# Two steps' products with the values issued together in causal attention, over three buffers of exponentials

## The reference

```python
scores = jnp.einsum('bqhd,bkhd->bhqk', q, k)
scores = scores + jnp.einsum('bqr,bkr->bqk', q_rope, k_rope)[:, None]
scores = scores / scale
scores = jnp.where(causal[None, None], -jnp.inf, scores)
w = jax.nn.softmax(scores, axis=-1)
attn = jnp.einsum('bhqk,bkhd->bqhd', w, v).reshape(Bb, Tt, D_MODEL)
return attn @ W_o
```

## Time and profile before

| | us |
|---|---|
| median of 3 runs | 2069.44 (2067.35 to 2071.24) |
| profiled execution, its own time | 2063.16 |
| its span, first to last instruction | 2061.4 |
| attention, first to last exponential | 235.6 to 1146.7 |
| TensorE busy over the span | 1628.2 |
| VectorE busy over the span | 1153.2 |
| ScalarE busy over the span | 876.3 |

### The profile page before, as it was taken

How to read it: one execution, slowest core, us unless ns; L and a number is a source line. 1 busy time by engine, 2 the same in 40 slices (tenths; PEclk the granted TensorE clock), 3 DMA queues, 4 the chain that set the end, 5 groups by cost and what they waited for, 6 DMA issues and landing times. The chain is left out here.

```text
span 2061.4 us, 32062 instructions
## 1 busy us (share of the span) xinstructions
PE 1628.2 (79%) x12596; PEld 758.6 (37%) x12596; DVE 1153.2 (56%) x3013; ACT 876.3 (43%) x1186; POOL 351.5 (17%) x414
## 2 busy tenths in 40 slices
PE   7954579999999999999999276401887967888889
PEld 5421122333333333333333152201343434566566
DVE  3815779787878778786870034500444565311466
ACT  2420245666666666666667103301454533311132
POOL 2512780000000000000000040174221200300011
PEclk9985799999999999999999686655999988999989
DMA  7487440303030120404000130025665410584011
GB/s 255 156 176 167 135 135 22 78 27 78 14 79 26 49 56 27 70 22 78 27 27 27 68 133 0 13 105 140 146 160 140 130 47 1 204 289 166 5 36 52
DMA packets 94213, 183.85 MB, mean 89 GB/s; under 512 B 12656, under 2 KB 60912, under 8 KB 93040
## 3 DMA queue, kind: packets, MB, share of 16 engines
q1 hardware_dynamic: 73024, 110.91, 21.1%
q0 software_dynamic: 19376, 68.41, 10.1%
q10 hardware_dynamic: 1664, 2.49, 0.3%
HBM read 123.31 MB, written 58.37 MB: 88 GB/s over the span
## 5 line engine op out<-in xcount | busy, mean ns | idle before, releaser
L885 ACT ACTIVATE at_pr<-ps 128x1024 f32<-128x1024 f32 (+3 forms) x640 | 546.7, 894 | 349.4 <-PE ps L825 220.3
L918 DVE TENSOR_REDUCE at_mx<-ps 128x1 f32<-128x512 f32 x768 | 489.1, 685 | 149.2 <-PE ps L777 141.0
L915 DVE CUSTOM_DVE_ANT_0 at_seen<-ps,later 128x384 bf16<-128x384 f32 (+3 forms) x512 | 229.2, 486 | 16.1 <-issue 10.7
L825 PE MATMUL ps<-bq,bk 64*128 64x512 f16 (+3 forms) x1280 | 224.0, 347 | 0.0
L822 PE MATMUL ps<-sqk 64*128 64x512 f16 (+3 forms) x1280 | 172.6, 348 | 13.4 <-DMA sqk<-at_mr 13.4
L822 PE MATMUL ps<-at_sqk 64*128 64x512 f16 (+3 forms) x1280 | 171.2, 346 | 6.4 <-DMA at_sqk<-at_mr 5.7
L777 PE MATMUL ps<-sqk 64*128 64x512 f16 (+3 forms) x640 | 120.7, 374 | 61.4 <-DVE at_mx L918 29.5
L719 POOL DMA_DIRECT2D d_o<-at_oc x32 | 17.3, 540 | 807.8 <-ACT at_oc L876 785.1
L801 PE MATMUL ps<-at_pr,vl 128*32 128x512 f32 (+3 forms) x1280 | 150.5, 542 | 0.0
L801 PE MATMUL ps<-at_pr,at_vl 128*32 128x512 f32 (+3 forms) x1280 | 150.0, 541 | 0.1
L777 PE MATMUL ps<-at_sqk 64*128 64x512 f16 (+3 forms) x640 | 114.7, 355 | 19.9 <-DVE at_mx L918 8.1
(11 more groups left out here) (264 smaller groups left out, 2367.7 us busy)
## 6 DMA issues: line engine op xcount, KB each, us to landing
mi_tz<-d_z SPq DMA_DIRECT2D x32, 1024.0 KB, 7.0
ex_w<-d_w POOLq DMA_DIRECT2D x23, 768.0 KB, 6.5
d_rows<-at_nil POOLq DMA_DIRECT2D x32, 379.5 KB, 3.0
ex_xr<-d_rows SPq DMA_DIRECT2D x23, 512.0 KB, 8.8
d_va<-st_va SPq DMA_DIRECT2D x8, 1024.0 KB, 4.9
d_o<-at_oc POOLq DMA_DIRECT2D x32, 256.0 KB, 2.3
at_pw<-in_w POOLq DMA_DIRECT2D x24, 256.0 KB, 3.1
d_w<-at_ph POOLq DMA_DIRECT2D x24, 256.0 KB, 2.4
```

Of the source, the lines that this page charges most:

```text
L825: ins = pe.matmul(ps[:, 2 * f + r, off:CH], g.bk[half[r], b, k], g.bq[half[r], b, q], start=False, stop=t < 0)
L885: act.activation(pr[:, n % 2, f, :, off:CH], ps[:, 2 * f:2 * f + 2, off:CH], ACT.Exp, scale=INV_SCALE).then_inc(exp_done[f], 1)
L915: ins = dve.tensor_tensor_reduce(seen[:, turn, r, 0:n], src, g.later[:, CH - n:CH], 1.0, LOWEST, ALU.add, ALU.max, dst)
L918: ins = dve.tensor_reduce(dst, src, AX.X, ALU.max)
```

## The change

`pr` gets a third buffer. A step's buffer is now the number of the step over all units, modulo three. TensorE issues no product with the values in odd steps; in an even step it issues those of the two steps before, one behind the other, in the place where the one of the step before stood. In step 0 these are the last two of the unit before. ScalarE waits for the product of three steps back. The spreading of the maxima and everything else stays.

```diff
+    PR = 3
...
-        pr = sb("pr", [P, 2, 2, 2, CH])
+        pr = sb("pr", [P, PR, 2, 2, CH])
...
-                                    pr[:, n % 2, h // 2, h % 2, off:CH], start=(kb == 0),
+                                    pr[:, (u * NS + n) % PR, h // 2, h % 2, off:CH], start=(kb == 0),
...
                     if s == 0 and not first:
+                        weighted(*before, NS - 2)
                         weighted(*before, NS - 1)
-                    if s >= 1:
+                    if s >= 2 and s % 2 == 0:
+                        weighted(grp, b, s - 2)
                         weighted(grp, b, s - 1)
...
                 if last:
+                    weighted(grp, b, NS - 2)
                     weighted(grp, b, NS - 1)
...
-                    act.wait_ge(pv_done[n % 2], u * (NS // 2) + n // 2 + 1)
+                    step = u * NS + n
+                    if step >= PR:
+                        act.wait_ge(pv_done[(step - PR) % 2], (step - PR) // 2 + 2)
...
-                        act.activation(pr[:, n % 2, f, :, off:CH], ps[:, 2 * f:2 * f + 2, off:CH], ACT.Exp,
+                        act.activation(pr[:, step % PR, f, :, off:CH], ps[:, 2 * f:2 * f + 2, off:CH], ACT.Exp,
```

## The result

| | before | after |
|---|---|---|
| median us | 2070.34 (4 runs, 2067.35 to 2080.03) | 2143.76 (4 runs, 2138.19 to 2150.14) |
| ratio | | 1.035 (95% interval 1.032 to 1.038) |
| profiled execution's span | 2061.4 | 2148.4 |
| attention, first to last exponential | 911.0 | 986.2 |

A forecast was written before the change was run, and what follows sets the result against it. TensorE and VectorE were taken to share the bound, step by step. Six middle units at +9.8 us give +59, the first +11, the last +12: +82 us, so 2151 us is predicted, range 2118 to 2193.

The forecast's parts named there:

- Price of the surroundings: TensorE in attention: pair to pair 1.18 us with only scores between; a second product behind the first costs 0.90.
- parts 1 to 3: Odd steps gain 0.01 to 0.13 us, even steps pay 0.90; middle unit +8.0 for wide pairs, +2.1 and +0.6 for narrower.
- part 4: Step 9, without maxima: transposition 0.5 us earlier, then 0.9 and 0.1 paid in step 10, +0.5 in all.
- part 5: Steps with short scores and no second pair, whose 256-wide product was not covered: together -1.3 us a middle unit.
- part 6: Transposition for the next unit starts 0.3 us earlier, the next unit's step 0 pays 0.2: taken -0.1.
- part 7: Third buffer of exponentials and ScalarE's wait three steps back: nothing is queued longer, cost 0.
- First unit: First of attention's eight units (one group of heads of one batch), first seven odd steps saturated: +11 us.
- Last unit: Attention's eighth unit, no maxima to make ahead: about +3 in steps 0 to 8, +9 from step 9, +12 us.
- Rival A: Borders of the products: half of 320 save 0.25 us each in switches, 40 us faster, 2029 us; chance 0.07.
- Rival B: Slack takes it up: TensorE's gain in odd steps balances the even steps' 0.90 us, no change, 2069; chance 0.04.
- Rival C: Second product pays its entire fixed part (+34, 2185 us) or granted clock falls (2177); chance 0.09 together with Rival D.
- Rival D: An exponential waits for its buffer and the scores behind it wait too, adding time; chance under 1 in 50.

The follow-up runs named there:

- the clean base: The changed kernel with its products put back, one in each step, third buffer kept: last unit 94.1 us, whole 2063.35 us, ratio to before 1.001.
- the kernels with both cuts: Kernels before and after, with reductions over 32 columns and exponentials over 128, the rest left out: 1979.30 and 1989.63 us, ratios to before 0.958 and 0.964.

## Why the prediction was right

The forecast was 2151 us, +82; measured 2143.76, +73, and attention +75.2. The kernel is slower by the mechanism named: the product was taken off VectorE's time, and ScalarE's in the last unit.

*Price of the surroundings.* Pair to pair 1.17 with nothing between (1.18 forecast), 2.16 over two products (2.21). The second product costs 2.16-1.31 = 0.85 us, its columns alone (0.86 in the forecast); with the border I had taken 0.90. So the border between two products costs nothing that shows. By the weight-load rule of the Trainium skill (TensorE: Matmul & The Clock Gate, Part 3), that a load overlaps running matmuls only where the row groups differ, I had put it at 0.1 us. The measurement decides against this use of it: both products use all rows, and the block of sixteen runs through.

*Odd and even steps (parts 1 to 3).* Forecast +0.80 a period with wide pairs, measured 0.72 to 0.77 in nine of ten and 0.80 in one: 0.85-0.14 = 0.71 and a little saturation. With 384 columns 0.68, 0.60 and 0.68 for 0.70; step 29 0.60 for 0.6. Together about 10.0 for 10.7.

*Step 9 (part 4).* +0.48 for +0.5. *Steps 15, 27, 35 (part 5).* -0.67, -0.02, -0.46, together -1.15 for -1.3. *End of a unit (part 6).* -0.2 for -0.1 (+0.54 in steps 37 and 38, -0.74 in 39 and the next unit's first). *Third buffer (part 7).* 0 for 0, by its own run. Middle unit: +9.1 for +9.8.

*First unit:* +10.9 for +11. That it fits so well is luck: by the scatter of this unit (139.9 and 141.3 with the old order, 150.8 and 149.2 with the new) the cost lies anywhere from 8 to 11, and the clock granted in it was 0.95 to 0.98 in all kernels, with no tie to the order.

*Last unit:* +10.0 against the clean base (+9.4 against the profile of before) for +12. This is the term furthest off. Steps 0 to 8 cost +2.9 for 3, its full periods 0.73 to 0.79 for 0.77, those with 384 columns 0.56 to 0.62 for 0.6. Too high were step 9 (0.48 for 0.6), the three periods before a masked step (0.62 for 0.77: the second half waits less), and above all the three short ones (-0.15 to -0.24 for +0.2). These had been estimated by the columns of the scores. In fact the short product taken out of an odd step gave back 0.15 to 0.24, and the one added behind it cost nothing, since TensorE waited for ScalarE there already before the change.

*Rival A, the switches.* A product that stands alone loses 0.25 us at its two borders by the earlier trace rows, and a pair of borders saved gave back 0.23 in the kernels with both cuts. By the Trainium skill (TensorEngine Tiling, Key Properties) a change of tiling mode drains TensorE; the trace agrees in that time is lost there, though no run shows that a drain is the reason. It does not decide, as the distance between pairs stays at 1.17. Even with that at 0.67 it did not: a middle unit still cost +2.7.

*Rival B* fell with the odd steps. *Rival C:* neither part happened; the second product paid no fixed part, and the granted clock of the middle units stayed at 1.00 with TensorE busy 87% (105.35 of 121.7). The 0.98 of the last unit, which I had read as a sign of idle spells, was the 3.4 us in the profile of before, in a unit that has TensorE busy 98%; with the change that unit had 1.00. *Rival D:* ScalarE's waits in the middle unit are for scores (L827, L832); none is for a product.

Two sums of the prediction are off and changed nothing. Part 5 writes 0.70 us for 0.57+0.11, which is 0.68. And the low end of the range does not follow from its reason: with a third of the 160 doubled blocks covered, 160/3 times 0.90 = 48 us would go, which leaves +34 (2103 us) and not the +50 (2118) that stands there.

One expected sign was too weak a test. I had said that the weight loads' waits for VectorE would be no smaller; they were equal (24.0 and 26.1), and would be equal too if nothing had been lost. The matmuls' own waits (12.6 for 2.8) told the two apart.

## What to carry to other kernels

Before work is moved off its place, ask what waits behind it: a product between two links of a round trip to another engine costs only what it exceeds the round trip by (0.14 us here), and nearly all of its time once it stands elsewhere (0.86). Measure a round trip by the distance between starts where nothing else stands between them (1.17 us here by VectorE, 2.00 by ScalarE), compare it with the distance over the work to be moved, and look for a second round trip behind the first. Work that stands where no round trip is running may be moved into one. That is where this change gained, in steps 15 and 35 (0.67 and 0.46 us) and at the unit's end.

## What had not been expected

Behind the product stood two walls, not one: with reductions over 32 columns a middle unit still cost +3.6, with exponentials cut too +2.7. What is left fits the fixed part of the way to VectorE and back: pair to pair is still 0.67 us with reductions of 32 columns, against 1.17 with 512. No run took this part away, so that it would bring the middle unit under its base is not shown. A busy share says little of such a loop: in a middle unit TensorE was at 95% before and VectorE at 80%, and shorter reductions alone took 9.0 off the 112.6 us.
